# Attention scores as 64-row products in both halves of the TensorE array, with four row banks and three score banks

## The chip, the cores and the metric

The kernel runs on one core of a Trainium2 chip. The metric is the device time of one execution in microseconds (us), lower is better. One core has five engines that run their own instruction streams and meet at semaphores: TensorE (PE in the rows; its weight loads are PEld), VectorE (DVE), ScalarE (ACT), GpSimd (POOL) and SyncE (SP), which here issues DMA transfers.

## What is computed

A small transformer block on an input x of 2 x 2048 tokens with 256 features: attention, a mixture of experts, a state-space scan, and the mixture of experts again, each on a layer norm of x and added to x. The change touches attention alone:

```python
Q = (x @ WQ + bQ).reshape(b, n, N_HEADS, D_K)          # 16 heads of 16
K = (x @ WK + bK).reshape(b, n, N_HEADS, D_K)
V = (x @ WV + bV).reshape(b, n, N_HEADS, D_K)
Qr = jnp.einsum('bnhd,dr->bnhr', Q, WQr)
Kr = jnp.einsum('bnhd,dr->bnhr', K, WKr)
scores = jnp.einsum('bnhr,bmhr->bnhm', Qr, Kr) / math.sqrt(RANK)   # 2048 x 2048 for each head
A = jax.nn.softmax(scores, axis=-1)
out = jnp.einsum('bnhm,bmhv->bnhv', A, V).reshape(b, n, d)
return out @ WO + bO
```

With two batches there are 32 heads in all, each with a 2048 x 2048 score matrix.

## The kernel before

The phases run one after the other. `phase_attention` (L446) takes the 32 heads in turn. A head's scores are cut into 64 tiles of 128 x 512, called steps (`STEPS`). Each score tile is computed twice by PE:

- `row_score` (L688): queries on the partitions, keys along the free axis, into one of three banks `pR` of PSUM. DVE takes the maximum of each row of 512 (L625). This is done one head ahead (`LEAD` = 16 steps more than that), since the maximum of a query must be known before its exponentials.
- `col_score` (L699): keys on the partitions, queries along the free axis, into one of three banks `pS`. ACT takes the exponential (L611) into `probs`.

Queries and keys were split into three bfloat16 parts by the phase before, and a score is the sum over six pairs of parts. A part has 16 rows, so the tiles `qs` and `ks` of a head hold 96 rows (`PAIR_ROWS`), the contraction of one product. Two more rows of `qs` carry the negated row maximum in two bfloat16 parts, against ones in `ks`, so the column product contracts over 98 rows and its result is already shifted.

`values` (L709) multiplies the exponentials of four steps with the head's values, augmented by a column of ones, as four float32 products with 17 columns each, in four column groups of the array (`pA[32 * c:...]`). It lags the exponentials by a group of 8 steps. At a head's second group, `combine` (L729) transposes the accumulated sums of the previous head into `pO`, and DVE's `normalise` (L647) divides. At the seventh group's end, `turn_maxima` (L739) transposes the maxima of the next head into another part of the same bank `pO`, DVE's `send` (L640) copies them out, and SP's `shift` (L525) moves them into the rows of `qs` by two transfers. SP's `load` (L519) brings a head's parts two heads ahead, twelve transfers of 64 KB each.

The order on PE is written out by hand in `head` (L752): for each step one column product and one row product, and after every four steps one half of the values of the group before. PE executes in that order, so a wait on one product holds all that stand behind it. A row product waits until DVE has finished with its bank (step k - 3), a column product until ACT has (step k - 3). The heads 1 to 27 are a loop of three heads for each turn; the first head and the last four are written out. Before the first head come the 64 row products of head 0 with nothing else beside them, and before those GpSimd's constants (L557 to L574), on which PE waits.

I call a **period** the work of four steps: four column products, four row products and one half of the values. A head has 16.

## Time and profile before

| what | us |
|---|---|
| median of 3 runs | 3359.72 (3358.65 to 3366.12) |
| the profiled execution: its own time | 3341.25 |
| its span, first to last instruction | 3339.5 |
| attention's row maxima (L625), first to last start | 135.6 to 1645.0 |
| attention's exponentials (L611), first to last start | 184.5 to 1694.3 |

Attention is thus some 1560 us of the span, and nearly half of the time. The page of the profile gives busy time by engine and by line; "busy" of PE is the union of its matmuls, whose ends are modelled, so matmuls that follow each other closely overlap in the records: one lasts 379 ns there, and the next starts 0.22 us after it. The numbers to read are therefore starts, not durations. In the timeline each row gives the start, the length, the engine, the line, the operation with its operands, how many were merged (xN), and in brackets the idle time of the engine before it with what ended it.

### The profile page before, as it was taken

To read this page: it belongs to the slowest core of one execution; us is meant where nothing else is said; L and a number is where in the kernel's file an instruction comes from. 1 tells how busy PE (TensorE), PEld (TensorE's weight loads), DVE (VectorE), ACT (ScalarE), POOL (GpSimd) and SP (SyncE) were. 2 spreads that over 40 slices of the span, in tenths; PEclk is the share of its full clock that TensorE was granted. 3 is DMA by queue.
4 is the path that set the end of the run, shared out by engine and by line. 5 is a ranking of instruction groups with operands and counts; after the bars stand their busy time and mean duration, and the time that the engine had idled before them with its cause. 6 is when DMAs were issued, how large, how long until landed. Compare 5 with 4: busy or idle time off the path is not lost. (4 is left out here: it accounts for less than half of the span.)

```text
span 3339.5 us, 53729 instructions
## 1 busy us (share of the span) xinstructions
PE 2734.7 (82%) x13598; PEld 1245.2 (37%) x13598; DVE 2410.0 (72%) x4101; ACT 1605.0 (48%) x3030; POOL 1066.8 (32%) x1044
## 2 busy tenths in 40 slices
PE   7799999999999999999975877745576676597772
PEld 4323233233323223233245466632122223446662
DVE  6798888888888888888617932238799997792223
ACT  3257676677767667677742321115544443231110
POOL 3300000000000000000020367773599995037772
PEclk9789999999999999999985989977799998599996
DMA  4600000000000000000211258841233331126886
GB/s 137 200 20 20 12 20 21 21 11 21 20 20 12 21 21 20 11 20 20 68 43 56 58 147 205 218 121 55 62 109 97 116 109 40 63 51 168 216 208 196
DMA packets 184546, 255.14 MB, mean 76 GB/s; under 512 B 26256, under 2 KB 139984, under 8 KB 184272
## 3 DMA queue, kind: packets, MB, share of 16 engines
q1 hardware_dynamic: 157936, 213.29, 21.2%
q0 software_dynamic: 24576, 37.77, 6.5%
q8 instruction: 112, 1.84, 0.2%
q14 instruction: 162, 1.33, 0.1%
q10 hardware_dynamic: 1760, 0.93, 0.1%
HBM read 189.53 MB, written 62.03 MB: 75 GB/s over the span
## 5 line engine op out<-in xcount | busy, mean ns | idle before, releaser
L625 DVE TENSOR_REDUCE att_mx<-att_pR 128x1 f32<-128x512 f32 x2048 | 1271.0, 683 | 196.0 <-PE att_pR L695 192.0
L611 ACT ACTIVATE att_probs<-att_pS 128x512 f32<-128x512 f32 x2048 | 1063.0, 604 | 502.2 <-PE att_pS L706 502.1
L695 PE MATMUL att_pR<-att_ks,att_qs 96*128 96x512 bf16 x2048 | 801.7, 392 | 15.9 <-POOL att_vh L573 14.6
L706 PE MATMUL att_pS<-att_qs,att_ks 98*128 98x512 bf16 x2048 | 782.4, 385 | 26.1 <-issue 20.4
L721 PE MATMUL att_pA<-att_probs,att_vh 128*17 128x512 f32 x4096 | 543.2, 602 | 0.3 <-ACT att_acc_sb L599 0.2
L578 POOL COPY att_vh<-all_v 128x256 f32 (+1 forms) x32 | 12.7, 400 | 1422.9 <-PE att_pA L721 1422.9
L706 PEld LDWEIGHTS att_pS<-att_qs,att_ks 98*128 98x128 bf16 x2048 | 199.4, 98 | 645.0 <-ACT att_probs L611 405.2
L2040 PE MATMUL sc_pY<-sc_hc,all_ident 128*128 128x512 f32 x512 | 273.8, 661 | 123.1 <-DVE sc_hc L1997 103.1
L695 PEld LDWEIGHTS att_pR<-att_ks,att_qs 96*128 96x128 bf16 x2048 | 201.2, 98 | 277.6 <-DVE att_mx L625 139.1
L1924 POOL TENSOR_TENSOR sc_bh<-ssm_du,sc_b 128x1024 f32<-128x1024 f32 x128 | 298.5, 2352 | 15.6 <-DVE sc_hc L1997 6.1
L1987 DVE TENSOR_TENSOR_SCAN sc_bh<-sc_pD,sc_carry,sc_bh 128x512 f32<-128x512 f32 x192 | 232.1, 1259 | 0.2 <-POOL sc_bh L1924 0.2
L2040 PEld LDWEIGHTS sc_pY<-sc_hc,all_ident 128*128 128x128 f32 x512 | 97.6, 205 | 274.6 <-DVE sc_hc L1997 141.0
L1957 ACT ACTIVATE sc_pD<-ssm_delta,ssm_negA 128x512 f32 x256 | 168.5, 684 | 48.9 <-DVE sc_bh L1987 48.8
L1372 DVE TENSOR_TENSOR f1e_hh<-f1e_sg,f1e_pG 96x256 f32<-96x256 f32 x64 | 26.7, 417 | 202.9 <-ACT f1e_sg L1328 202.9
L1372 DVE TENSOR_TENSOR f2e_hh<-f2e_sg,f2e_pG 96x256 f32<-96x256 f32 x64 | 26.7, 417 | 201.9 <-ACT f2e_sg L1328 201.9
L721 PEld LDWEIGHTS att_pA<-att_probs,att_vh 128*17 128x17 f32 x4096 | 68.2, 95 | 173.2 <-issue 84.9
L1281 POOL DMA_INDIRECT expert_sum<-f1e_y,f1e_idx x64 | 101.8, 1591 | 15.3 <-issue 11.5
L1281 POOL DMA_INDIRECT expert_sum<-f2e_y,f2e_idx x64 | 101.7, 1589 | 14.2 <-issue 10.8
L1997 DVE TENSOR_TENSOR sc_hc<-sc_bh,sc_pC 128x1024 f32<-128x1024 f32 x88 | 104.8, 1191 | 0.5 <-DVE sc_bh L1987 0.5
L1963 ACT ACTIVATE sc_carry<-sc_bh 128x2 f32<-128x2 f32 x96 | 19.8, 207 | 165.9 <-DVE sc_bh L1987 165.9
L1934 POOL TENSOR_TENSOR sc_hc<-sc_bh,sc_c 128x1024 f32<-128x1024 f32 x40 | 94.1, 2353 | 10.5 <-DVE sc_bh L1987 10.5
L1320 ACT ACTIVATE f1e_xT<-f1e_pX 128x256 f32<-128x256 f32 x64 | 24.5, 383 | 122.2 <-PE f1e_pX L1424 122.2
(292 smaller groups left out, 3475.1 us busy)
## 6 DMA issues: line engine op xcount, KB each, us to landing
sc_b<-scan_rows SPq DMA_DIRECT2D x128, 256.0 KB, 3.3
expert_sum<-att_zeros SPq DMA_DIRECT2D x4, 4224.0 KB, 20.2
att_qs<-query_parts SPq DMA_DIRECT2D x192, 64.0 KB, 2.2
att_ks<-key_parts SPq DMA_DIRECT2D x192, 64.0 KB, 2.1
f1e_wg<-in_w_gate SPq DMA_DIRECT2D x64, 192.0 KB, 2.9
f1e_wu<-in_w_up SPq DMA_DIRECT2D x64, 192.0 KB, 3.4
f1e_wd<-in_w_down SPq DMA_DIRECT2D x64, 192.0 KB, 4.1
f2e_wg<-in_w_gate SPq DMA_DIRECT2D x64, 192.0 KB, 3.0
```

The costliest lines, as they stand in the source:

```text
L611: act.activation(probs[:, k % (2 * HALF), :], pS[:, (s + k) % 3, :], ACT.Exp, scale=float(DK) ** -0.5).then_inc(expd, 1)
L625: dve.tensor_reduce(mx4[s][:, k // QC, k % QC:k % QC + 1], pR[:, (s + k) % 3, :], AX.X, ALU.max).then_inc(maxed, 1)
L695: pe.matmul(pR[:, (s + k) % 3, :], qs[s][0:PAIR_ROWS, t * P:(t + 1) * P], ks[s][0:PAIR_ROWS, c * GROUP:(c + 1) * GROUP], start=True, stop= ...
L706: pe.matmul(pS[:, (s + k) % 3, :], ks[s][:, t * P:(t + 1) * P], qs[s][:, c * GROUP:(c + 1) * GROUP], start=True, stop=True).then_inc(col_s ...
L721: mm = pe.matmul(pA[32 * c:32 * c + DK + 1, :], vh[s][:, t, :], probs[:, (HALF * g + j) % (2 * HALF), :], start=(t == 0), stop=(t == KT - ...
L1281: pool.indirect_dma_start(out=sums[s % 2][:, :], out_offset=bass.IndirectOffsetOnAxis(ap=idx[s][:, 0:1], axis=0), in_=y[s][:, :], in_offse ...
L1924: pool.tensor_tensor(bh[k % H_RING][:, :, :], du[:, :, col(b, k)], b_sb[s][:, :].rearrange("p (a n) -> p a n", a=1).to_broadcast([P, DC, S ...
L1934: pool.tensor_tensor(hc[hc_slot(k)][:, :, :], bh[k % H_RING][:, :, :], c_sb[i % C_RING][:, :].rearrange("p (a n) -> p a n", a=1) .to_broad ...
L1957: act.activation(pD[:, i % D_RING, :], delta[:, c, col(b, k)], ACT.Exp, scale=negA[:, c, n:n + 1]).then_inc(decay_ready, 1)
L1987: dve.tensor_tensor_scan(bh[k % H_RING][:, c, :], pD[:, i % D_RING, :], bh[k % H_RING][:, c, :], 0.0 if k < STATES else carry[:, c, n:n + ...
L1997: dve.tensor_tensor(hc[hc_slot(k)][:, :, :], bh[k % H_RING][:, :, :], pC[:, i % 2:i % 2 + 1, :].to_broadcast([P, DC, SPAN]), ALU.mult).the ...
L2040: mm = pe.matmul(pY[:, c, :], ident[:, :], hc[hc_slot(k)][:, c, :], start=(n == 0), stop=(n == STATES - 1))
```

## The change

Part by part:

- The order of the pairs of parts is changed, so that the four pairs of the first two parts stand in the first 64 rows. The row product contracts over those 64 rows alone (`MAX_ROWS`); the maximum is a shift and need not be exact. The column product is made of two products that accumulate in the same bank: one of 64 rows and one of the other 34 (`REST_ROWS`: 32 and the two shift rows).
- Each head's operands are held twice: `qs`, `ks` as before, and `q2`, `k2` with the first 64 rows on partitions 64 to 127 and the rest on 0 to 33. A step's products so use either the lower or the upper 64 rows of the array: for an even step the row product the lower half and both column halves the upper one, for an odd step the other way round.
- PE's order is in turns of two steps: row product k, first halves of columns k and k + 1, second halves of both, row product k + 1. After every second turn comes one half of the values, as before.
- `pR` has four banks instead of three. `pS` keeps three, and the bank `pO` is given up: `combine` and `turn_maxima` now stand together before step 56 and take one place of the ring of `pS`, so that the bank has to be free of `normalise` and `send` by step 58.
- `load` issues 24 transfers for a head, `shift` four. GpSimd clears three more small tiles to one before PE may start.

The core of the diff:

```diff
+Q_PARTS = (0, 1, 0, 1, 2, 0)
+K_PARTS = (0, 0, 1, 1, 0, 2)
+MAX_PARTS = 4
+MAX_ROWS = DK * MAX_PARTS
...
+REST_ROWS = ROWS - MAX_ROWS
...
-    LOADS = 2 * len(Q_PARTS)
+    LOADS = 2 * 2 * len(Q_PARTS)
+    SHIFTS = 2 * SHIFT_ROWS
+    RING, ROW_RING = SLOTS, 4
+    SIDE = STEPS - HALF
+    PLACES = STEPS + 1
...
-        pR = m.ps("pR", [P, 3, BANK])
-        pS = m.ps("pS", [P, 3, BANK])
+        pR = m.ps("pR", [P, ROW_RING, BANK])
+        pS = m.ps("pS", [P, RING, BANK])
...
-        pO = m.ps("pO", [P, BANK])
...
+        def place(k):
+            return k + (k >= SIDE)
+        SIDE_PLACE = place(SIDE) - 1
+        STEP_AT = {place(k): k for k in range(STEPS)}
+        def bank(s, at):
+            return pS[:, (2 * s + at) % RING, :]
...
+                        at = (DK * r + MAX_ROWS) % P
+                        sp.dma_start(twin[at:at + DK, :],
+                                     side[part, bass.ds(v(n * DK), DK), :]).then_inc(qk_in[s], 16)
...
+                pool.memset(k2[s][PAIR_ROWS - MAX_ROWS:REST_ROWS, :], 1.0).then_inc(consts, 1)
...
-                    pe.wait_ge(maxed, v(STEPS * n + k - 2))
+                    pe.wait_ge(maxed, v(STEPS * n + k - ROW_RING + 1))
...
+            def free_bank(n, at):
+                before, n_before = at - RING, n
+                if before < 0:
+                    if start(n):
+                        return
+                    before, n_before = before + PLACES, n - 1
+                if before == SIDE_PLACE:
+                    if not start(n_before):
+                        pe.wait_ge(normed, v(n_before))
+                    if not (isinstance(n_before, int) and n_before == NH - 1):
+                        pe.wait_ge(nmT_ready, v(n_before + 2))
+                else:
+                    pe.wait_ge(expd, v(STEPS * n_before + STEP_AT[before] + 1))
...
+            def col_half(n, s, k, half):
+                c, t = k % QC, k // QC
+                q, kk = ((q2[s], k2[s]), (qs[s], ks[s]))[(k + half) % 2]
+                at = MAX_ROWS * (1 - k % 2)
+                rows = slice(at, at + (MAX_ROWS, REST_ROWS)[half])
+                mm = pe.matmul(bank(s, place(k)), kk[rows, t * P:(t + 1) * P],
+                               q[rows, c * GROUP:(c + 1) * GROUP], start=not half, stop=bool(half))
...
             def head(n, s, turn, ahead):
                 for g in range(GR):
-                    for j in range(HALF):
+                    for j in range(0, HALF, 2):
                         k = HALF * g + j
-                        col_score(n, s, turn, k)
+                        if k == SIDE:
+                            free_bank(n, SIDE_PLACE)
+                            if not start(n):
+                                combine(n - 1, s)
+                            if ahead >= 1:
+                                turn_maxima(n + 1, s)
...
+                        if rows:
+                            free_row(n_r, s_r, turn_r, k_r)
+                            row_score(n_r, s_r, k_r)
+                        free_col(n, s, turn, k)
+                        col_half(n, s, k, 0)
+                        free_col(n, s, turn, k + 1)
+                        col_half(n, s, k + 1, 0)
+                        col_half(n, s, k, 1)
+                        col_half(n, s, k + 1, 1)
+                        if rows:
+                            free_row(n_r, s_r, turn_r, k_r + 1)
+                            row_score(n_r, s_r, k_r + 1)
+                        if j % QC == 2:
+                            last_values(n, s, g, j // QC)
```

On PE, one period (four steps) in the loop of heads of the kernel before. The names in brackets are those of the first user of a semaphore number: `qkv_wt_done` is here DVE's count of finished maxima (`maxed`), `qkv_wf_done` ACT's of finished exponentials (`expd`). "ISA" rows compute a register for the wait behind them.

```order
L706 MATMUL att_pS<-att_qs2,att_ks2 128x512 [waits qkv_wf_done]
L693 ISA
L695 MATMUL att_pR<-att_ks0,att_qs0 128x512 [waits qkv_wt_done]
L704 ISA
L706 MATMUL att_pS<-att_qs2,att_ks2 128x512 [waits qkv_wf_done]
L693 ISA
L695 MATMUL att_pR<-att_ks0,att_qs0 128x512 [waits qkv_wt_done]
```

Here stand two steps, and a period has two such pieces before its values. The same two steps in the changed kernel, one turn (`q22` and `k22` are the tiles `q2` and `k2` of slot 2):

```order
L723 ISA
L730 MATMUL att_pR<-att_ks0,att_qs0 128x512 [waits qkv_wt_done]
L746 ISA
L760 MATMUL att_pS<-att_q22,att_k22 128x512 [waits qkv_wf_done]
L746 ISA
L760 MATMUL att_pS<-att_qs2,att_ks2 128x512 [waits qkv_wf_done]
L760 MATMUL att_pS<-att_qs2,att_ks2 128x512
L760 MATMUL att_pS<-att_q22,att_k22 128x512
L723 ISA
L730 MATMUL att_pR<-att_k20,att_q20 128x512 [waits qkv_wt_done]
```

Six products take the place of four, with as many waits. The wait of the second column product now stands ahead of the second half of the first one, and ahead of the turn's last row product.

On DVE, at the seventh group of a head in the loop, the kernel before copies the turned maxima out and goes on with row maxima; the sums are normalised elsewhere, between row maxima of the second group:

```order
L645 CAST att_nmT<-att_pO 32x128 [waits qkv_x_in0]
L624 ISA
L625 TENSOR_REDUCE att_mx40<-att_pR 128x1 [waits qkv_blocks]
```

In the changed kernel both stand in a row there (`qkv_blocks` is the count of row products, `qkv_var_ready` that of combined sums):

```order
L677 CAST att_nmT<-att_pS 32x128 [waits qkv_x_in0]
L681 ISA
L682 RECIPROCAL att_rden<-att_pS 128x16 [waits qkv_var_ready]
L684 ISA
L686 ISA [waits qkv_v_done]
L686 TENSOR_TENSOR all_a<-att_pS,att_rden 128x256
L656 ISA
L657 TENSOR_REDUCE att_mx40<-att_pR 128x1 [waits qkv_blocks]
```

The reciprocal and the product moved behind the copy, and PE's step 58 waits for them, since they read a bank of the ring `pS`.

## Rows read from the trace of the kernel before

**Rows 1.** Page, part 5: line, engine, operands, xcount, busy us, mean ns, idle.

```profile
L625 DVE TENSOR_REDUCE att_mx<-att_pR 128x1 f32<-128x512 f32 x2048 | 1271.0, 683 | 196.0 <-PE att_pR L695 192.0
L611 ACT ACTIVATE att_probs<-att_pS 128x512 f32<-128x512 f32 x2048 | 1063.0, 604 | 502.2 <-PE att_pS L706 502.1
```

**Rows 2.** Stretches: length, busy us of PE, PEld, DVE, ACT, POOL; PEclk, DMA, GB/s.

```profile
137.00:183.00 46.00, 44.15 (x76) 7.77 (x75) 45.26 (x79) 0.00 (x0) 0.00 (x0) 0.50 0.65 213
1020.00:1060.00 40.00, 39.95 (x232) 12.52 (x225) 35.33 (x62) 28.63 (x57) 0.40 (x1) 1.00 0.08 21
1667.00:1697.00 30.00, 26.65 (x157) 5.41 (x157) 0.00 (x0) 24.15 (x48) 0.00 (x0) 1.00 0.40 134
```

**Rows 3.** Timeline of one period in mid-attention: start us, length us, engine, line, operation.

```profile
805.57 0.39 PE L706 MATMUL att_pS<-att_qs,att_ks 98*128 98x512 bf16 x1
...
806.00 2.06 ACT L611 ACTIVATE att_probs<-att_pS 128x512 f32<-128x512 f32 x4 [0.77 <-PE att_pS L706]
...
806.22 2.48 DVE L625 TENSOR_REDUCE att_mx<-att_pR 128x1 f32<-128x512 f32 x4 [0.35 <-PE att_pR L695]
...
807.11 0.38 PE L695 MATMUL att_pR<-att_ks,att_qs 96*128 96x512 bf16 x1
...
807.42 1.05 PE L721 MATMUL att_pA<-att_probs,att_vh 128*17 128x512 f32 x8
...
808.41 0.39 PE L706 MATMUL att_pS<-att_qs,att_ks 98*128 98x512 bf16 x1
```

**Rows 4.** Timeline of the last head, column products without row products.

```profile
1662.61 0.11 PEld L706 LDWEIGHTS att_pS<-att_qs,att_ks 98*128 98x128 bf16 x2 [0.85 <-ACT att_probs L611]
1662.61 0.82 PE L706 MATMUL att_pS<-att_qs,att_ks 98*128 98x512 bf16 x3
...
1663.69 0.39 PE L706 MATMUL att_pS<-att_qs,att_ks 98*128 98x512 bf16 x1 [0.26 <-ACT att_probs L611]
```

**Rows 5.** Timeline of the last head: two period starts.

```profile
1655.08 0.82 PE L706 MATMUL att_pS<-att_qs,att_ks 98*128 98x512 bf16 x3
...
1657.52 0.82 PE L706 MATMUL att_pS<-att_qs,att_ks 98*128 98x512 bf16 x3
```

**Rows 6.** Timeline of the scan's first stage: 128-row and 64-row products, and ACT.

```profile
2256.01 0.59 PE L1801 MATMUL si_pB<-ssm_xnT,si_wbc 128*96 128x512 f32 x1
...
2256.64 0.59 ACT L1688 ACTIVATE si_bc_hi<-si_pB 96x512 bf16<-96x512 f32 x1 [1.91 <-PE si_pB L1801]
...
2257.93 0.59 PE L1808 MATMUL si_pD<-si_low,si_wdp 64*128 64x512 f32 x1
...
2258.55 0.69 ACT L1700 ACTIVATE si_size<-si_pD,si_bcol 128x512 f32<-128x512 f32 x1 [0.33 <-PE si_pD L1808]
```

**Rows 7.** Timeline of the start of attention: DVE's maxima back to back.

```profile
150.51 2.47 DVE L625 TENSOR_REDUCE att_mx<-att_pR 128x1 f32<-128x512 f32 x4
```

**Rows 8.** Timeline at the turn of the maxima, PE, DVE and SP.

```profile
794.48 0.22 PE L744 MATMUL att_pO<-att_identb,att_nm 128*32 128x128 bf16 x1
...
794.86 0.28 DVE L645 CAST att_nmT<-att_pO 32x128 bf16<-32x128 f32 x1
...
795.17 1.14 SPq L529 DMA_DIRECT2D att_qs<-att_nmT  x2
```

**Rows 9.** Lines 649 and 653 in 190 to 1600 us: min/median/max ns.

```profile
L649 DVE RECIPROCAL att_rden<-att_pO x29: 244/246/249, 241.8 to 1575.8; 128x16 f32<-128x16 f32 x29
L653 DVE TENSOR_TENSOR all_a<-att_pO,att_rden x29: 423/425/425, 242.2 to 1576.1; 128x256 f32 x27, 128x256 f32<-128x256 f32 x2
```

**Rows 10.** Timeline: SP's loads of head 1, GpSimd's last long constant, PE's first product.

```profile
131.74 2.73 SPq L522 DMA_DIRECT2D att_qs<-query_parts  x6
...
132.87 1.80 POOL L571 MEMSET att_ks<- 2x2048 bf16 x1
...
134.91 0.61 PE L695 MATMUL att_pR<-att_ks,att_qs 96*128 96x512 bf16 x1 [14.61 <-POOL att_vh L573]
```

**Rows 11.** Issues in 200 to 1600 us: transfer, xcount, KB, median us to landing.

```profile
att_qs<-att_nmT SPq DMA_DIRECT2D x58, 4.0 KB, 2.0
```

More of the change, by code:

```diff
@@ L660, in head @@
                 if ahead >= 1:
-                    maxima(n + 1, s1, range(LEAD, 2 * LEAD))
-                if not start(n):
-                    normalise(n - 1)
-                if ahead >= 1:
-                    maxima(n + 1, s1, range(2 * LEAD, STEPS))
+                    maxima(n + 1, s1, range(LEAD, STEPS))
                     negate(n + 1, s1)
```

102 lines of the change are left out of this document (51 added, 51 removed).

## The prediction

> **What bounds the kernel now.** I read the page's groups first, then stretches of the trace, then the timeline of a single period, because shares of busy time can't separate the engines here. In mid-attention (1020 to 1060 us) PE is busy 39.95 of 40 us, DVE 35.33, ACT 28.63, at a granted clock of 1.00, 2.4 GHz [rows 2]. The timeline shows why [rows 3]: within a period PE's eight bf16 products start 0.22 us apart (805.57 to 807.11 is seven slots of 0.22), the values start 0.31 us after the last product (0.09 more than a slot) and the next period's first column product 0.99 us after that. So a period is 7 x 0.22 + 0.31 + 0.99 = 2.84 us, all of it PE's. DVE and ACT both wait for PE in it: DVE sits idle 0.35 us before its four maxima and ACT 0.77 us before its four exponentials. DVE alone can take a maximum every (2.47 - 0.68) / 3 = 0.60 us [rows 1, 7], which is 2.39 us for a period, and ACT an exponential every (2.06 - 0.60) / 3 = 0.49 us [rows 1, 3], 1.95 us. At first sight a faster PE has 0.45 us of 2.84 to win until DVE is the bound.
>
> How many periods count: heads 0 to 29 run 16 each with both kinds of products, head 30 twelve, together 492; the last 20 (four of head 30, 16 of head 31) have no row products.
>
> **The change, part by part.**
>
> *The PE slots.* If the products in the lower and the upper half of the array overlap fully, a turn of two steps is three slots for each half: 0.66 us instead of four slots, 0.88. A period then needs 5 slots between its first and its last pair, plus the offset d of the second product of a pair: 5 x 0.22 + d + 0.31 + 0.99 = 2.40 + d. No row shows two products in two row halves. The nearest from one side are the values [rows 3]: eight matmuls in four column groups end within 1.05 us, where bf16 products in one position take 0.22 us each and float32 ones of the same length 0.59 alone [rows 6]; the four groups run side by side with next to no offset. From the other side, products in one position start 0.22 us apart [rows 3], and half of that, 0.11, is an even spread of the two streams; two weight loads in a row also end within 0.11 us [rows 4]. I take d = 0.015, near the column groups, with 0 and 0.11 as ends, and both ends go into the range. That a 64-row product delivers no earlier than a 128-row one is shown by the scan's first stage: ACT starts 0.63 us after the last 128-row product started and 0.62 after the last 64-row one [rows 6].
>
> *The wait for ACT, in its new place.* This is the term that decides. The ring `pS` still has three banks, so column k + 1 of a turn may start only when exponential k - 2, the first of the turn before, has ended. Before, that was harmless: column k + 3 stood six slots, 1.32 us, behind column k. The price of the round trip is in the last head, where nothing but columns stands in PE's way: the first column product starts at 1662.61, the fourth, which reuses its bank, at 1663.69 [rows 4]. That is 1.08 us, made of 0.43 until ACT starts (805.57 to 806.00 [rows 3]), 0.60 of exponential [rows 1] and 0.05 to release PE. In the new order column k is complete only with its second half, which starts one slot and an offset into the turn (0.22 + d), so bank k comes free at 0.22 + d + 1.08 = 1.31 us, while PE arrives at the first half of column k + 3 in slot 4, at 0.88 us. PE stands still for 0.43 us. Queued behind that wait in PE's order are the second half of column k + 2, that of k + 3, the turn's last row product, and the values, whose own inputs are long ready. After the release one slot and one offset pass until the last row product. The period is
>
> 0.22 + 0.015 + 1.08 + 0.22 + 0.015 + 0.31 + 0.99 = 2.85 us,
>
> against 2.84 before. Everything that the halves win (2.84 - 2.42 = 0.42) goes back into that one wait. It comes once a period, not twice: the first turn after the values finds its banks free, since the values cover 0.99 us, and ACT then has no backlog (its four exponentials take 2.06 of 2.85). With slots of 0.22 known to about 0.002, the difference is +0.01 us, times 492 = **+5 us**; with d = 0 it is -0.02 (-10 us), with d = 0.11 it is +0.20 (+98 us).
>
> *DVE and the fourth row bank.* The rows of a period start at 0, 0.45, 0.66 and 1.55 us. DVE takes them in 2.39 of 2.85 us and isn't late; the fourth bank lets PE run ahead, but PE is not held by rows in either kernel. Nothing.
>
> *The last 20 periods.* Before, without row products, a period was 1657.52 - 1655.08 = 2.44 us [rows 5]. In the new order the row products are not in the chain; the last slot is then column k + 3's second half, and a period keeps its 2.84 us. The old order gains in this stretch from the row products' absence, and the new one, held by ACT, does not: 20 x 0.40 = **+8 us**.
>
> *Combine and turn before step 56.* Their matmuls are the same, at another place, so PE's time for them stays. New is that step 58 waits for `normalise` and `send`. From the turn's matmul it is 0.38 us to the copy [rows 8], 0.28 for that, 0.25 and 0.42 for the reciprocal and the product [rows 9], and about 0.1 for two releases: 1.43 us. Step 59 has to wait for exponential 56 anyway, which comes free 1.31 us after the first product of the turn, itself one short slot (some 0.15) behind the turn's matmul: 1.46 us. Hidden, by 0.03, less than I can know; if not, each 0.1 us costs 3 us over 31 heads.
>
> *Transfers.* SP issues 24 loads for a head instead of 12, with some 40 steps, 28 us, until they are needed; at no more than 0.57 us for an issue (two in 1.14 us [rows 8]) they take 14. The four shift transfers take 2.3 us to issue and 2.0 to land [rows 11]: ready 4.3 us after 795.17, or 5.0 after the turn's matmul at 794.48 [rows 8], while 0.15 and two periods, 5.85 us, pass until the next head's first column. Hidden, by 0.85 us. If that cover were gone, all of PE would wait at each head's start.
>
> *The start.* PE's first product comes right after GpSimd's last constant [rows 10]. Three more memsets of two partitions, at 1.80 us and some 0.05 of release each, move it by **+5.5 us**, to 140.4. The loads of head 0 were issued by 131.74, where those of head 1 begin, at 0.46 each [rows 10]; twelve more end at 137.3 and land some 2 us later, 139.3. The memsets hide them, by 1 us.
>
> **The sum**: +5 + 8 + 5.5 = +18.5 us. Against the profiled execution's own 3341.25 us that is 3359.8; the median of the runs stands 18.5 us higher, at 3359.72, and by chance by as much, so the time to expect as a median is **3378 us**.
>
> The Trainium skill speaks for a larger effect in TensorEngine Tiling (Array Packing), Theoretical Speedup: a contraction of 64 rows or less in two row tiles gives up to 2x. Read so, the period would be 2.42 us and attention 0.42 x 492 = 207 us shorter, short of the wait that the rows put in the way. The same page's section PSUM Bottleneck warns that tiling speeds up TensorE and not the emptying of PSUM, which is that wait; no run here shows either yet.
>
> **The rivals.**
>
> *The halves overlap in part.* Each pair then takes longer than a slot, as it would if two products that write 128 partitions each share a path. Against it stands that four column groups show no slowdown [rows 3]. If a pair takes 1.3 slots, 0.286 us, the chain's two slots cost 0.13 us more for each of 492 periods, +65 us: 3443. An estimate from the Trainium skill lands there: TensorE: Matmul & The Clock Gate, "Measured speedup vs the span model", gives 3.07x for four row-packed products instead of 4, a factor of 1.30 on a slot; no run here shows it.
>
> *They don't overlap at all*, so that the change doesn't do what it says: 12 products in a row for a period, 11 x 0.22 + 1.30 = 3.72 us, +0.88 x 492 = +433, with the other terms +447: 3806. Against it: the column groups.
>
> *The wait is shorter than I make it, and the change wins.* All hangs on 1.08 us in the chain. If an exponential starts earlier after a 34-row product, or going from values to 64-row products costs less than the 0.99 and 0.31 us of today, each 0.05 us off a period is worth 25 us: 3353 at 0.05, 3328 at 0.1. If the wait vanished altogether, DVE would be the bound: 64 x 0.60 + 1.6 for its other work of a head (0.95 of it in [rows 8, 9], the rest my estimate for the negation) is 40.0 us, 2.50 for a period, -0.34 x 492 = -167, with the start 3205. The starts in [rows 3, 4, 6] speak against both.
>
> *The clock.* In the start PE runs at 0.50 of its clock, 1.2 GHz, with one product for each 0.60 us; in the last head, with pauses of 0.3 us, it stays at 1.00 [rows 2]. A period with pauses of 0.43 us lies nearer to the last head. If part of the time fell to 1.2 GHz, a period there would take some 4.5 us; at 3% of the periods that is +25 us: 3403.
>
> **How the numbers follow.** The forecast, 3366 to 3395 around 3378, has 0.50. The same mechanism with a smaller d or a slightly shorter chain ends within 0.2% of before, 3353 to 3366: 0.15. Partial overlap, a large offset or a lower clock, 3395 to 3450: 0.13. No overlap: 0.05. Faster: 0.12 for a chain shorter by 0.05 to 0.1 and 0.05 for no wait at all, 0.17. So 0.17 faster, 0.15 same, 0.68 slower, where 0.2% (6.7 us) is about what a measurement of this kernel can tell from no change. The range goes from 3325 to 3445 and leaves out no overlap (0.05), the vanished wait (0.05), and the outer tails (some 0.07).
>
> **What the profile after would show.** Right: starts of PE's products in pairs, 0.22 us from pair to pair; a pause of about 0.4 us once in a period, before the first half of an odd column (the second, not the first turn), with ACT's exponential named as releaser; a period of 2.85 us; attention's first product near 140.4 us; the last head's periods at 2.84 us instead of 2.44. Wrong: twelve even starts in a period (no overlap), a period of 2.5 with DVE busy throughout (no wait), a clock clearly under 1.00 in mid-attention, or a wait on the maxima or on the shift transfers at a head's first column.

## The result, and the profile of the changed kernel

The change makes the kernel slower by about half a percent: a median of 3374.81 us (18 runs, 3351.63 to 3387.10) against 3352.25 us for the kernel before (18 runs, 3341.65 to 3366.12). The ratio is 1.0057, with a 95% interval of 1.0038 to 1.0075, so some 19 us (the two medians alone differ by 22.6). The profiled execution of the changed kernel took 3379.68 us, its span is 3377.9 us, and the mean granted clock is 0.901 (before 0.906).

The two groups of part 5 of its page that answer to [rows 1]:

```profile
L657 DVE TENSOR_REDUCE att_mx<-att_pR 128x1 f32<-128x512 f32 x2048 | 1267.0, 682 | 174.0 <-PE att_pR L730 173.5
L643 ACT ACTIVATE att_probs<-att_pS 128x512 f32<-128x512 f32 x2048 | 1111.1, 595 | 473.9 <-PE att_pS L760 473.7
```

A maximum costs what it cost before, 682 ns (683), and an exponential 595 ns (604). The middle stretch of [rows 2] (length, busy us of PE, PEld, DVE, ACT, POOL; clock, DMA share, GB/s):

```profile
1020.00:1060.00 40.00, 36.30 (x285) 9.84 (x281) 34.90 (x61) 29.75 (x56) 0.40 (x1) 1.00 0.10 26
```

In mid-attention PE was busy 39.95 of 40 us; now it is busy 36.30, and the clock still is 1.00, 2.4 GHz. PE has been relieved, and no other engine does more for it: DVE runs 61 instructions in the stretch (62 before) and ACT 56 (57). Busy shares cannot say where the time went; a period in the timeline can (start us, length us, engine, line, operation, in brackets the idle time before it and its releaser):

```profile
1020.25 0.39 PE L730 MATMUL att_pR<-att_ks,att_qs 64*128 64x512 bf16 x1
1020.25 0.39 PE L760 MATMUL att_pS<-att_q,att_k 64*128 64x512 bf16 x1
1020.47 0.38 PE L760 MATMUL att_pS<-att_qs,att_ks 64*128 64x512 bf16 x2
...
1020.69 0.38 PE L760 MATMUL att_pS<-att_q,att_k 34*128 34x512 bf16 x1
...
1020.89 2.17 ACT L643 ACTIVATE att_probs<-att_pS 128x512 f32<-128x512 f32 x4 [0.65 <-PE att_pS L760]
1020.91 0.38 PE L730 MATMUL att_pR<-att_ks,att_qs 64*128 64x512 bf16 x1
...
1021.55 0.39 PE L760 MATMUL att_pS<-att_qs,att_ks 64*128 64x512 bf16 x2 [0.26 <-ACT att_probs L643]
...
1022.09 1.05 PE L777 MATMUL att_pA<-att_probs,att_vh 128*17 128x512 f32 x8
1023.07 0.39 PE L730 MATMUL att_pR<-att_ks,att_qs 64*128 64x512 bf16 x1
```

Products start in pairs, and the two of a pair start within a hundredth of a microsecond. Pairs are 0.22 us apart: 1020.25, 1020.47, 1020.69, 1020.91. Then the first half of the turn's odd column, the fifth pair, is missing where it was due, at 1021.13, and comes at 1021.55, with ACT's exponential as its releaser. The values follow at 1022.09 and the next period at 1023.07: 2.82 us, where [rows 3] have 2.84. The 0.42 us at 1021.13 is the whole gain of the halves, spent standing still. The waits of PE's products between 200 and 1500 us say the same of all periods (waiting group, releaser: us in total, times, longest us):

```profile
PE att_pS L760 <- ACT att_probs L643: 103.9, 401, 0.3
PE att_pR L730 <- issue: 19.3, 8, 2.8
PE att_pS L760 <- DVE all_a L686: 8.7, 26, 0.3
```

Some 435 periods lie in this stretch, so 401 waits of 0.26 us are about one for each of them. A wait counts from the end of the last record, 0.38 us long, and so is 0.16 shorter than the pause between starts. The third line will matter below.

**Where the 19 us are.** The extra time comes from attention, which can be cut at ACT's first and last exponential, and at the 492 periods with row products:

| part of attention | before, us | after, us | difference | forecast |
|---|---|---|---|---|
| until the first exponential | 184.5 | 192.2 | +7.7 | +5.5 |
| 492 periods with rows, with the heads' other steps | 1461.4 | 1466.3 | +4.9 | +5 |
| last 20 periods | 48.4 | 57.8 | +9.4 | +8 |
| last exponential | 1694.3 | 1716.3 | +22.0 | +18.5 |

The spans of the two profiled executions differ by 38 us, 16 of them behind attention, in code that the change doesn't touch (1645.2 against 1661.6 us). In the profiles of all kernels shown here that part varies between 1642.7 and 1671.8 us whatever attention does, so those 16 us are no effect of the change; the ratio over all runs agrees with the +22 within its interval.

**What the busy stretch doesn't show.** The loop of heads goes round once for three heads (these turns of the loop are not the turns of two steps), and at each of its eight turns PE stands still for 2 to 3 us, with "issue" as the releaser (20.4 us in all before, 19.3 after). Behind six of these pauses in the kernel before, and behind all eight in the changed one, the granted clock falls to 0.50, 1.2 GHz, for some microseconds, and PE's products start 0.43 us apart. In full_96, an experiment below, it falls behind one of the eight. Eight microseconds around the end of such a pause, in the kernel before, in the changed kernel and in full_96 (columns as above):

```profile
944.00:952.00 8.00, 7.38 (x23) 2.06 (x24) 3.71 (x6) 3.50 (x7) 0.00 (x0) 0.57 0.38 94
1099.00:1107.00 8.00, 7.42 (x46) 1.88 (x48) 5.33 (x9) 4.34 (x8) 0.31 (x1) 0.79 0.42 112
1095.00:1103.00 8.00, 7.14 (x39) 2.45 (x40) 5.80 (x10) 5.17 (x11) 0.40 (x1) 1.00 0.45 117
```

An undisturbed head of the loop takes 46.44 us before and 46.66 after. What the 27 heads of the loop take beyond that is 33.8 us before and 33.7 after, so the turns and the slow stretches behind them cost both kernels the same in these two executions and are no part of the +22. In full_96 they cost 20. Whether that is chance isn't shown.

### The profile page after: what moved, and what is told of

Same layout as the page of the kernel before. It is cut to its first block and busy times, and to the rows that moved or that the text cites. A ratio compares the mean times of both kernels' runs of the same rounds, so it can differ in the third digit from the quotient of the medians.

```text
span 3377.9 us, 58896 instructions
## 1 busy us (share of the span) xinstructions
PE 2634.0 (78%) x15646; PEld 1164.2 (34%) x15646; DVE 2403.7 (71%) x4101; ACT 1653.7 (49%) x3030; POOL 1072.9 (32%) x1047
## 5 line engine op out<-in xcount | busy, mean ns | idle before, releaser
L643 ACT ACTIVATE att_probs<-att_pS 128x512 f32<-128x512 f32 x2048 | 1111.1, 595 | 473.9 <-PE att_pS L760 473.7
L760 PE MATMUL att_pS<-att_q,att_k 64*128 64x512 bf16 (+1 forms) x2048 | 708.1, 383 | 9.8 <-DVE all_a L686 9.8
L760 PE MATMUL att_pS<-att_qs,att_ks 64*128 64x512 bf16 (+1 forms) x2048 | 407.2, 386 | 127.7 <-ACT att_probs L643 127.5
L730 PE MATMUL att_pR<-att_ks,att_qs 64*128 64x512 bf16 x1024 | 403.5, 394 | 40.2 <-POOL att_vh L605 20.2
L730 PE MATMUL att_pR<-att_k,att_q 64*128 64x512 bf16 x1024 | 399.4, 390 | 0.0
L730 PEld LDWEIGHTS att_pR<-att_ks,att_qs 64*128 64x128 bf16 x1024 | 97.1, 95 | 517.6 <-DVE att_mx L657 409.1
L760 PEld LDWEIGHTS att_pS<-att_q,att_k 64*128 64x128 bf16 (+1 forms) x2048 | 192.4, 95 | 102.4 <-DVE att_nmT L677 22.3
L760 PEld LDWEIGHTS att_pS<-att_qs,att_ks 64*128 64x128 bf16 (+1 forms) x2048 | 100.3, 94 | 368.5 <-ACT att_probs L643 367.6
```

The costliest lines, as they stand in the source:

```text
L643: act.activation(probs[:, k % (2 * HALF), :], bank(s, place(k)), ACT.Exp, scale=float(DK) ** -0.5).then_inc(expd, 1)
L730: pe.matmul(pR[:, k % ROW_RING, :], q[rows, t * P:(t + 1) * P], kk[rows, c * GROUP:(c + 1) * GROUP], start=True, stop=True).then_inc(row_s ...
L760: mm = pe.matmul(bank(s, place(k)), kk[rows, t * P:(t + 1) * P], q[rows, c * GROUP:(c + 1) * GROUP], start=not half, stop=bool(half))
```

## Experiments

All are built from the changed kernel unless said otherwise. Ratios are to the kernel before, run on the same chip. The theory is the one of the prediction: the halves overlap, and the three score banks, each held until an exponential has ended, hand the gain back. The rivals are that the halves overlap little or not at all, that DVE's maxima or the row banks set the period, and that PE itself does.

### A fourth score bank: four_banks

The score ring has four banks and the row ring three, so the sum of banks stays as it is; combine and turn write one bank of the ring and take four places of it, so that the ring starts anew with the same bank.

```diff
-    RING, ROW_RING = SLOTS, 4
+    RING, ROW_RING = 4, 3
...
-    PLACES = STEPS + 1
+    PLACES = STEPS + RING
...
-            return k + (k >= SIDE)
...
-        SIDE_PLACE = place(SIDE) - 1
+            return k + RING * (k >= SIDE)
...
+        SIDE_PLACE = SIDE + 2
...
-            return pS[:, (2 * s + at) % RING, :]
+            return pS[:, at % RING, :]
```

> The changed kernel with four score banks and three row banks instead of the reverse; combine and turn take one bank of four before step 56. Theory (the halves' gain goes into the wait for an exponential, since a turn needs the banks of the turn just before it): with a fourth score bank a turn's columns wait for exponentials two turns back, so the pause of 0.4 us in each period is gone, PE's period is 5 slots of 0.22 + 0.31 + 0.99 = 2.40 us, DVE's 2.39, with the coupling of the two some 2.45 to 2.50. 492 periods x -0.35 is -170 us, +10 for step 58's wait on the normalising: ratio to the kernel before 0.950 to 0.965. Rival (the halves do not shorten PE's work when they overlap, or the row maxima hold PE): period stays at 2.8 or more, ratio 1.00 to 1.01.

Measured: 0.9654 (0.9622 to 0.9685), 3240.17 against 3354.61 us. The median period falls from 2.82 to 2.475 us. PE's timeline of one period:

```profile
931.76 0.39 PE L730 MATMUL att_pR<-att_ks,att_qs 64*128 64x512 bf16 x1
...
932.43 0.38 PE L730 MATMUL att_pR<-att_ks,att_qs 64*128 64x512 bf16 x1
...
932.65 0.38 PE L762 MATMUL att_pS<-att_qs,att_ks 64*128 64x512 bf16 x2
...
932.94 0.39 PE L730 MATMUL att_pR<-att_k,att_q 64*128 64x512 bf16 x1
...
934.24 0.39 PE L730 MATMUL att_pR<-att_ks,att_qs 64*128 64x512 bf16 x1
```

The pause before the odd column is gone: its pair stands at 932.65, one slot after 932.43. What comes late now is the period's last row product: due one slot later, at 932.86, it starts at 932.94, and these 0.08 us are what 2.475 has over PE's own work (2.39, below). Such a pause is too short to show between the ends of products, but the weight loads name who they wait for (300 to 1300 us; us in total, times, longest us):

```profile
PEld att_pR L730 <- DVE att_mx L657: 419.4, 982, 1.7
```

So the score ring was what took the gain, and with it out of the way DVE's maxima and their three banks come next. From the changed kernel's ratio of 1.0057 to 0.9654 is some 135 us, where 160 were expected, though the period came as expected; the rest is in the part of a head that belongs to no period. From one copy of the sums to the next a head takes 42.53 us, of which 16 x 2.475 = 39.60 are periods, leaving 2.93, against 46.66 - 16 x 2.823 = 1.49 in the changed kernel.

### Shorter exponentials: short_exp_after and short_exp_before

The exponential covers 256 of the 512 columns, in the changed kernel and, with the same edit, in the kernel before.

```diff
-                        act.activation(probs[:, k % (2 * HALF), :], bank(s, place(k)), ACT.Exp,
+                        act.activation(probs[:, k % (2 * HALF), 0:256], bank(s, place(k))[:, 0:256], ACT.Exp,
```

> The changed kernel with exponentials over 256 of 512 columns (the other half of the tile stays at one, so half of the attention weights is left out). It shortens ACT's instruction by some 0.27 us, from 0.60 to about 0.33. Theory: the chain of a period contains one whole exponential, so a period shrinks by 0.27 us, to 2.55: -0.27 x 492 = -133 us on the changed kernel, ratio to the kernel before about 0.966. Rival (PE's own work, its mode changes or DVE set the period of 2.83): no change.

> The same shorter exponentials in the kernel before (half of the attention weights left out). Theory: there PE's slots set the period and the exponential is outside the chain: period stays at 2.84, only the last 20 periods shrink by some 0.2 us, -4 us, ratio 0.998 to 1.00. Rival (ACT's round trip also bounds the kernel before): some -100 us.

In the changed kernel: 0.9697 (0.9661 to 0.9733), 3258.16 us, and a period of 2.61 us instead of 2.82. Timeline of ACT and PE:

```profile
1053.21 0.66 ACT L643 ACTIVATE att_probs<-att_pS 128x256 f32<-128x256 f32 x2 [1.08 <-PE att_pS L761]
...
1053.65 0.39 PE L761 MATMUL att_pS<-att_qs,att_ks 64*128 64x512 bf16 x2
...
1056.26 0.39 PE L761 MATMUL att_pS<-att_qs,att_ks 64*128 64x512 bf16 x2
```

In the kernel before: 0.9983 (0.9953 to 1.0013), 3356.20 us, and a period of 2.84 us as ever:

```profile
1020.42 0.39 PE L707 MATMUL att_pS<-att_qs,att_ks 98*128 98x512 bf16 x1
...
1020.85 1.69 ACT L611 ACTIVATE att_probs<-att_pS 128x256 f32<-128x256 f32 x4 [1.14 <-PE att_pS L707]
...
1023.26 0.39 PE L707 MATMUL att_pS<-att_qs,att_ks 98*128 98x512 bf16 x1
```

An exponential of 256 columns is about 0.21 us shorter than one of 512 (382 against 595 ns on average; 0.27 was expected, and a period of 2.55), and the period of the changed kernel is 0.213 us shorter: one exponential stands in each of its periods, whole, and it is the one before the pair at 1053.65. In the kernel before none stands in it; PE starts its products at the same 2.84 us while ACT idles 1.14 us. This pair of runs shows the term on which the forecast hung, and it does so with the banks left as they are.

### Shorter maxima: short_max_after and short_max_four

The maxima read 256 of the 512 columns of a row bank, in the changed kernel and in the one with four score banks.

```diff
-                    dve.tensor_reduce(mx4[s][:, k // QC, k % QC:k % QC + 1], pR[:, k % ROW_RING, :],
+                    dve.tensor_reduce(mx4[s][:, k // QC, k % QC:k % QC + 1], pR[:, k % ROW_RING, 0:256],
```

> The changed kernel with row maxima over 256 of 512 columns (the other half of the keys is left out of the maximum). DVE's instruction shrinks from 0.60 us to 0.33. Theory (ACT's round trip sets the period, DVE does not): period stays at 2.82; only the start, 80 row products at DVE's pace, shrinks by some 0.17 us each, -14 us: ratio about 1.00. Rival (row banks or DVE take part in the period): period clearly under 2.8.

> The same shorter row maxima (half of the keys left out of the maximum) with four score banks. Theory: there DVE (4 x 0.60) and its three row banks set the 2.475 us of a period; without them PE's 5 slots + 1.30 = 2.40 us are left: -0.07 x 492 = -37, start -14: some -50 us on the kernel with four score banks, ratio about 0.95. Rival (ACT or PE sets 2.475): only the start's 14 us.

In the changed kernel: 1.0025 (0.9996 to 1.0054), 3355.65 us. Its stretch in mid-attention (columns as above):

```profile
1020.00:1060.00 40.00, 36.30 (x285) 9.85 (x281) 23.21 (x61) 29.75 (x56) 0.40 (x1) 1.00 0.15 41
```

DVE works 23.21 instead of 34.90 us in it, and PE and ACT do exactly what they did, 36.30 and 29.75. The period stays 2.823 us; the little that the kernel gains is at its start, where DVE's maxima stand alone (first exponential at 176.5 instead of 192.2 us, 3.1 of which are there before the first product, in the scatter of one execution). With four score banks the same edit gives 0.9426 (0.9380 to 0.9472), 3159.57 us, and a period of 2.39:

```profile
1026.87 0.39 PE L730 MATMUL att_pR<-att_ks,att_qs 64*128 64x512 bf16 x1
...
1027.97 0.38 PE L730 MATMUL att_pR<-att_k,att_q 64*128 64x512 bf16 x1
...
1029.26 0.39 PE L730 MATMUL att_pR<-att_ks,att_qs 64*128 64x512 bf16 x1
```

Five slots of 0.22 (1026.87 to 1027.97) and 1.29 until the values have gone through: this is PE with nothing in its way, the 2.40 + d of the prediction with d next to nothing. Against four_banks the time is some 76 us less where 50 were expected: 40 are the periods, and nearly 20 come from the part of a head outside of them, which falls from 2.93 to 2.31 us, the rest from the start. The three limits of a period are now measured one by one: PE 2.39, DVE with three row banks 2.475, the score ring of three 2.82.

### Do the halves overlap? one_half and six_full_height

Two ways to take the overlap away. In one_half every product reads the lower 64 rows; in six_full_height a turn has the same six products, with 96 or 98 rows each (the column scores are then added twice). The edit of one_half:

```diff
-                q, kk = ((qs[s], ks[s]), (q2[s], k2[s]))[k % 2]
-                rows = (slice(0, MAX_ROWS), slice(MAX_ROWS, 2 * MAX_ROWS))[k % 2]
+                q, kk, rows = qs[s], ks[s], slice(0, MAX_ROWS)
...
-                q, kk = ((q2[s], k2[s]), (qs[s], ks[s]))[(k + half) % 2]
-                at = MAX_ROWS * (1 - k % 2)
+                q, kk = ((qs[s], ks[s]), (q2[s], k2[s]))[half]
+                at = 0
```

and that of six_full_height:

```diff
+                q, kk, rows = qs[s], ks[s], slice(0, PAIR_ROWS)
...
+                q, kk, rows = qs[s], ks[s], slice(0, ROWS)
```

> The changed kernel with all score products in the lower 64 rows of the array, same number, same order, same banks. Theory: products in one half cannot overlap, a period is 11 slots of 0.22 + 1.30 = 3.7 us, +0.87 x 492 = +430 us on the changed kernel, ratio to the kernel before 1.13. Rival (the overlap of starts in the trace is only in the records and gives no time): ratio stays near 1.006.

> The changed kernel's order of six products a turn, but each over the full height: 96 rows for the row products, 98 rows twice for each column product (the scores are doubled, the shift too, so the weights are not the reference's). Like one_half it cannot overlap; unlike it, it uses the full height. If one_half stayed at 1.2 GHz because its products use half of the array, this one runs at a granted clock of 1.00 and a period of 11 x 0.22 + 1.30 = 3.70 us: ratio 1.13, the price of the missing overlap alone. Rival (six products in a row keep the clock down for another reason, such as the start at 1.2 GHz): period 7.07 us and ratio 1.63 again.

six_full_height came out as expected: 1.1313 (1.1242 to 1.1384), 3794.09 us, a period of 3.69 us.

```profile
1100.37 0.39 PE L729 MATMUL att_pR<-att_ks,att_qs 96*128 96x512 bf16 x1
...
1104.06 0.39 PE L729 MATMUL att_pR<-att_ks,att_qs 96*128 96x512 bf16 x1
```

Twelve products in a row cost 0.86 us more a period than the pairs do, even with the pairs' pause. Together with the five slots of 0.22 us in short_max_four this says that the overlap is whole. one_half missed its number by far: 1.6358 (1.6295 to 1.6421), 5496.14 us instead of some 3790. A stretch in mid-attention and the timeline of a period:

```profile
1020.00:1060.00 40.00, 40.00 (x115) 9.69 (x113) 15.33 (x23) 12.55 (x24) 0.00 (x0) 0.50 0.00 0
```

```profile
2019.13 0.60 PE L729 MATMUL att_pR<-att_ks,att_qs 64*128 64x512 bf16 x1
...
2026.19 0.60 PE L729 MATMUL att_pR<-att_ks,att_qs 64*128 64x512 bf16 x1
```

PE is busy without a break, 40.00 of 40 us, and its granted clock is 0.50, 1.2 GHz, all through attention. Its products stand 0.43 us apart, twice the 0.22, and the period of 7.06 us (2019.13 to 2026.19) is near twice the twelve-product period at full clock (2 x 3.69 = 7.38). The run says nothing against the overlap, but its ratio mixes two effects, and that is why six_full_height was run: there the same stretch has

```profile
1020.00:1060.00 40.00, 40.00 (x224) 13.14 (x217) 28.87 (x48) 22.73 (x43) 0.40 (x1) 1.00 0.12 34
```

with PE as busy and the clock at 1.00. Why the short products in one half alone stay at 1.2 GHz is open; the two kernels have the same six products a turn in the same order, and differ in the rows of a product and the tiles that it reads.

### All of the change but the halves: full_products and full_96

Both go back to one product for each column and each row, column and row in turn, and keep everything else: banks, the place of combine and turn, the transfers, the memsets. In full_products the row products keep their 64 rows, in full_96 they have 96 as before.

```diff
-                        free_col(n, s, turn, k)
-                        col_half(n, s, k, 0)
-                        free_col(n, s, turn, k + 1)
-                        col_half(n, s, k + 1, 0)
-                        col_half(n, s, k, 1)
-                        col_half(n, s, k + 1, 1)
...
+                        for i in range(2):
+                            free_col(n, s, turn, k + i)
+                            col_full(n, s, k + i)
+                            if rows:
+                                free_row(n_r, s_r, turn_r, k_r + i)
+                                row_score(n_r, s_r, k_r + i)
```

> The changed kernel with the halves undone: one column product of 98 rows and one row product of 64 rows for each step, alternating as in the kernel before; banks, ring, place of combine and turn, transfers and memsets as changed. Theory: period 2.83 us again (8 PE slots + 1.30), so all that this kernel loses is the start (+7 us) and the wait of step 58 on the normalising (column 58 is reached 1.0 us after the turn, the bank is free 1.5 us after it: 0.5 x 31 = +15 us): ratio 1.005 to 1.008, as slow as the changed kernel. Rival (the halves themselves, with their mode changes, lose the time of the changed kernel): period 2.83 and ratio 1.000 to 1.002.

> The halves undone as in full_products, now with row products of 96 rows, so that no product of 64 rows is left and PE's score products are all of one kind. Banks, ring, place of combine and turn, transfers and memsets stay as changed. If the 0.32 us slots of full_products came from alternating 64-row and 98-row products, they are 0.22 again here and the period is 2.83 us; the start (+7) and step 58's wait (0.5 x 31 = +15) remain: ratio 1.005 to 1.008. Rival (something in the new banks or ring costs the 0.10 us a slot): ratio 1.12 again.

full_products missed: 1.1203 (1.1112 to 1.1293), 3767.56 against 3346.69 us, a period of 3.55. The reason is in the timeline, in the spacing of PE's products:

```profile
1021.21 0.39 PE L767 MATMUL att_pS<-att_qs,att_ks 98*128 98x512 bf16 x1
1021.53 0.39 PE L730 MATMUL att_pR<-att_ks,att_qs 64*128 64x512 bf16 x1
```

They start 0.32 us apart instead of 0.22, and each stands next to one of another height. With 96 rows in place of the 64, full_96 is back at 0.22 (1019.62 to 1019.84) and at a period of 2.83:

```profile
1019.62 0.39 PE L766 MATMUL att_pS<-att_qs,att_ks 98*128 98x512 bf16 x1
...
1019.84 0.38 PE L729 MATMUL att_pR<-att_ks,att_qs 96*128 96x512 bf16 x1
...
1022.45 0.39 PE L766 MATMUL att_pS<-att_qs,att_ks 98*128 98x512 bf16 x1
```

So each step between a score product that fits one half and one that spans both costs 0.10 us; seven such slots are the 0.71 us between the two periods. The step from the last score product to the values, which span both halves too, shows no such price: it is 0.31 us after a 64-row product (1023.46 to 1023.77 in full_products, 1021.78 to 1022.09 in the changed kernel) as after a 96-row one [rows 3]. The Trainium skill has the rule without a number, in TensorEngine Tiling (Array Packing), Key Properties, "Mode switching requires drain"; between score products the runs agree with it; whether the 0.31 us before the values hold such a price in every kernel, they can't tell.

full_96 is the clean undoing: 1.0048 (1.0027 to 1.0069), 3370.11 against 3351.69 us. Everything around the halves costs half a percent, as much as the whole change, whose interval overlaps with it. In its trace the start is 5.2 us longer than before (first exponential 189.7 us), the period is 2.833 and a head 47.03 us. The halves take 0.01 off a period, and 0.37 off a head (46.66) of which 0.16 are its periods, some 11 us over all heads, and they give 8 of it back in the last 20 periods, 57.8 instead of 49.9 us. The sums of the two profiled executions don't show this, since the turns of the loop cost full_96 14 us less (see above): its 492 periods with rows and the heads' other steps took 1462.1 us, against 1466.3.

### What bounds the kernel with four banks: four_values_between, four_pool_negate, four_early_start

Built on four_banks. The first sets half of the values between the two turns of the last group, so that PE has work while the side step's results are under way:

```diff
-                        if j % QC == 2:
+                        if j == 6 or j == (0 if g == GR - 1 else 2):
                             last_values(n, s, g, j // QC)
```

> Four score banks, and in a head's last group the first half of the values stands after steps 56 and 57 instead of after 58 and 59, so that it covers step 58's wait for the normalising (0.7 us in the trace with four banks). Theory: -0.7 x 31 = -22 us on the kernel with four score banks, ratio to the kernel before about 0.959. Rival (DVE's sum for a head is the bound, so a wait moved comes back elsewhere): no change, 0.965.

Measured: 0.9650 (0.9619 to 0.9681), 3233.32 us, which is the rival's number and not to be told from four_banks, and a head of 42.45 instead of 42.53 us. Right after the side step the row products of this kernel stand like this:

```profile
930.07 0.39 PE L730 MATMUL att_pR<-att_k,att_q 64*128 64x512 bf16 x1
...
930.67 0.39 PE L730 MATMUL att_pR<-att_ks,att_qs 64*128 64x512 bf16 x1 [0.21 <-DVE att_mx L657]
```

0.60 us apart, which is a maximum's pace [rows 7]. The wait moved from one instruction to another: after the side step DVE is behind, and PE follows it. Then what shortens a head is work taken from DVE. four_pool_negate leaves DVE the reduction to a head's maxima and has GpSimd do the two negations:

```diff
-                dve.tensor_scalar(nm[:, 0, :], mx[:, :], -1.0, None, ALU.mult).then_inc(nm_hi, 1)
...
+                pool.tensor_tensor(nf[:, :], zeros[:, 0:KT], mx[:, :], ALU.subtract).then_inc(nm_hi, 1)
...
+                pool.tensor_tensor(nm[:, 0, :], zeros[:, 0:KT], mx[:, :], ALU.subtract).then_inc(nm_hi, 1)
...
+                pool.tensor_tensor(nm[:, 1, :], nf[:, :], nm[:, 0, :], ALU.subtract).then_inc(nm_ready, 1)
```

> Four score banks, and the two negations of the maxima on GpSimd instead of DVE. Theory after four_values_between (which moved the wait and won nothing): with four banks DVE's sum for a head is what bounds, 64 x 0.60 and its other work, so taking 0.4 us of instructions with their gaps (0.65 us) from it gives -0.65 x 31 = -20 us on four_banks: ratio 0.959. Rival (a wait of PE at the side place bounds the head): no change, or slower by GpSimd's longer way.

Measured: 0.9617 (0.9571 to 0.9663), 3226.30 us. The interval overlaps with that of four_banks, but the trace shows the step: an undisturbed head of the loop takes 42.09 us instead of 42.53, each time, 0.44 less where I had expected 0.65. Work off DVE shortens a head, work moved on PE doesn't.

four_early_start adds to this an earlier first product: DVE writes the three constants that GpSimd had got in addition, and ACT's queue issues head 0's second copies.

```diff
-                pool.memset(k2[s][PAIR_ROWS - MAX_ROWS:REST_ROWS, :], 1.0).then_inc(consts, 1)
...
+                dve.memset(k2[s][PAIR_ROWS - MAX_ROWS:REST_ROWS, :], 1.0).then_inc(acc_clear, 1)
...
+                    act.dma_start(twin[at:at + DK, :], side[part, 0:DK, :]).then_inc(qk_in[0], 16)
```

> four_pool_negate, and the three added memsets on DVE, which is idle at the start, and the twelve added loads of head 0 through ACT's queue. Theory: PE's first product comes 5.5 us earlier, at 134.9 us: -5.5 us, ratio 0.957. Rival (the loads of head 0 hold the start): it stays at 139 us, -1 us.

Measured: 0.9581 (0.9526 to 0.9637), 3219.36 us, the lowest ratio of the kernels here that leave nothing out, 4.2% under the kernel before; its interval overlaps with that of four_pool_negate. The first product:

```profile
138.41 0.58 PE L745 MATMUL att_pR<-att_ks,att_qs 64*128 64x512 bf16 x1 [17.88 <-DMA att_k<-key_parts]
```

It starts 4.2 us earlier than in the changed kernel, but 1.9 of these are the earlier start of the whole phase in this execution. Counted from attention's first memset, the first product comes after 8.8 us before, 14.3 in the changed kernel and 12.1 here: 2.3 of the 5.6 us that the memsets cost are won back. The releaser is no longer GpSimd but the last load. Behind the memsets the loads of the second copies were the next thing to wait for.

## Why the prediction was right, step by step

Direction and size came out: a ratio of 1.0057 where +18.5 us are 1.0055. The median of 3374.81 is near the 3378 in part by luck: the 3359.72 that the sum started from was the median of three runs, and that of 18 is 3352.25. A ratio, too, can come from errors that cancel, so each step is set beside its measurement.

**The halves overlap: right.** Pairs are 0.22 us apart, six_full_height prices their absence at 0.86 us a period, and the offset d is about 0.004 us, less than the 0.015 I took and at the column groups' end of my range, not at 0.11. The partial overlap of the rivals, 1.3 slots, is out: in short_max_four five slots are 1.10 us.

**The wait for ACT: right, and shown.** It stands where it was put, once in a period, before the odd column of the second turn, for 0.42 us (forecast 0.43). short_exp_after shortens the period by the exponential's own 0.21, and four_banks removes it. The period is 2.823 us instead of 2.85: d is smaller by 0.011 in both of its places. That is -0.01 us to before instead of +0.01, for 492 periods -5 us instead of +5. A term of the sum with the wrong sign, of small size, and its range included it.

**Combine and turn before step 56: the step that failed.** I called the wait of step 58 on `normalise` hidden behind the wait of step 59 on its exponential, by 0.03 us, and put the term at nothing. It isn't hidden. PE and DVE at this place of the changed kernel:

```profile
996.18 1.11 PE L787 MATMUL att_pS<-att_comb,att_acc_sb 128*128 128x68 f32 x8
...
997.22 0.23 PE L793 MATMUL att_pS<-att_identb,att_nm 128*32 128x128 bf16 x1
997.38 0.39 PE L730 MATMUL att_pR<-att_ks,att_qs 64*128 64x512 bf16 x1
...
998.75 0.38 PE L760 MATMUL att_pS<-att_q,att_k 64*128 64x512 bf16 x1 [0.33 <-DVE all_a L686]
998.87 0.49 PE L760 MATMUL att_pS<-att_qs,att_ks 64*128 64x512 bf16 x2
...
999.50 1.05 PE L777 MATMUL att_pA<-att_probs,att_vh 128*17 128x512 f32 x8
1000.49 0.39 PE L730 MATMUL att_pR<-att_ks,att_qs 64*128 64x512 bf16 x1
```

Step 58 is released 1.53 us after the turn's matmul, by the normalised head (`all_a`, 26 such waits in the third line of the waits above), and not 1.43. That alone would be 0.06 to 0.1. What I had missed is which column waits. In other periods the first half of the even column goes ahead with the row product, and only the odd column waits; from that release to the values it is 0.54 us (1021.55 to 1022.09). Here the even column itself waits, one slot more stands behind it, and it is 0.75 us (998.75 to 999.50). My own numbers would have shown it: a release of step 58 at 1.43 us puts step 59 one slot later, at 1.65, and not at the 1.46 that I compared it with. The period from 997.38 to 1000.49 is 3.11 us, 0.29 over the others. The combine and turn themselves take 1.20 us (996.18 to 997.38), where the time of a head outside of its 16 periods was 1.11 in all before. Together a head spends 1.49 us outside of its 16 x 2.823 instead of 1.11 outside of its 16 x 2.833, +0.38, over the 29 heads that combine **+11 us** where I had put 0. With the -5 of the periods this gives +6. Head by head, the measured +4.9 is: 27 heads of the loop at +0.22, +5.9; the two behind them, +1.1; the twelve periods of head 30, -0.6; the turns of the loop, -0.1; and head 0, which has no sums to combine, -1.5 (44.71 against 46.20 us), which I haven't taken apart. So the +5 of the sum came out by luck: a term with the wrong sign and one put at nothing made up for each other. I had written that the cover was thinner than I could know, and priced it at 3 us for 0.1, but took the side that costs nothing.

**The last 20 periods: right.** +9.4 us against +8. The last head's period, from first pair to first pair, is 2.87 us (forecast 2.84):

```profile
1670.32 0.39 PE L760 MATMUL att_pS<-att_q,att_k 64*128 64x512 bf16 x1
...
1673.19 0.39 PE L760 MATMUL att_pS<-att_q,att_k 64*128 64x512 bf16 x1
```

**The start: right in kind.** The first product is released by GpSimd's last constant, as forecast:

```profile
140.56 1.80 POOL L603 MEMSET att_k<- 2x2048 bf16 x1
...
142.59 0.60 PE L730 MATMUL att_pR<-att_ks,att_qs 64*128 64x512 bf16 x1 [20.18 <-POOL att_vh L605]
```

It comes at 142.59 us, 7.7 after the 134.91 of [rows 10]. The three memsets are 5.6 of it; the other 2.1 were there before attention's first memset, in a phase that the change doesn't touch, and are scatter of one execution. The loads were hidden, as I said, and by little: in the changed kernel the last of head 0's loads is issued at 138.81 us and landed 2.2 us later, 1.6 us before the first product. With the memsets gone, in four_early_start, the loads hold the start.

**DVE and the fourth row bank, the transfers, the clock: right.** short_max_after changes no period; no wait on the shift transfers shows up at a head's start; the clock in mid-attention stays at 1.00. Behind the turns of the loop it does fall, which the prediction didn't look for, but in both kernels and at the same cost (33.8 and 33.7 us with the turns). Of the rivals, the vanished wait (3205 us) is nearly what four_banks makes true, at 3240: the period I gave for it, 2.50, is 2.475 there. Its own sum has a slip: 3359.7 - 167 + 5.5 is 3198; 3205 holds the +8 of the last 20 periods as well.

## What to carry to other kernels

Count the depth of a ring of buffers in units of the new order, not of the old: a turn that fills two banks before it completes the first needs a bank more than one that fills them singly, or a whole round trip of the consumer enters the loop. Before a faster producer is built, write down the one wait that each buffer's reuse implies, from first use to release, and compare it with the time the faster producer takes to come back. When a dependent step is moved in front of a group, ask which instruction of the group waits, and how many stand behind it.

## What the runs showed of the hardware

- A change from a 64-row to a 98-row bf16 product and back costs 0.10 us each way (0.32 against 0.22 us slots in full_products and full_96), where products in different halves, or of 96 and 98 rows, follow one another without it. From a 64-row or a 96-row product to the values, in four column groups, it is 0.31 us alike.
- Products of 64 or 34 rows in the lower and the upper half start within a hundredth of a microsecond and run at full rate side by side, 0.22 us a pair.
- With 64-row products in the lower half alone PE is busy 40.00 of 40 us at a granted clock of 0.50, for all of attention, while the same order of 96- and 98-row products, and the pairs with their pauses, run at 1.00. What in the one kernel keeps the clock down is open.
- At a turn of the loop PE stands still for 2 to 3 us, and behind it the granted clock is often at 0.50 for some microseconds: after six of eight turns before the change, eight of eight after it, one of eight in full_96. With the pauses this is 34, 34 and 20 us of attention, and a stretch in the middle of a loop's body shows none of it.
